# Folding the logits of a pair of tiles by two transposes and an add on VectorE

## What is computed

```python
x = x + 0.5 * ffn(layernorm(x));  x = x + attn(layernorm(x));  x = x + 0.5 * ffn(layernorm(x))

def ffn(input, weight, bias, centroids, assignments):      # 64 clusters
    dots = softmax(x @ centroids.T / 0.1, axis=-1)
    hits = dots > 0.01
    query_sel = any(hits, axis=1);  cluster_sel = any(hits, axis=0)
    row_sel = cluster_sel[assignments]
    out = where(query_sel[:, None] & row_sel[None, :], x @ weight.T + bias, 0)

def attn(x, Wq, bq, Wk, bk, Wv, bv):                       # 32 heads of 32, 8 of them for k and v
    scores = einsum('bsdh,bseh->bsde', q, k) / sqrt(32)    # per token, over the heads
    out = einsum('bsde,bseh->bsdh', softmax(scores, axis=-1), v)
```

## Time and profile before

| | us |
|---|---|
| median of 3 runs | 1257.59 |
| lowest and highest run | 1253.8, 1264.04 |
| span of the profiled execution | 1253.4 |
| TensorE busy | 1224.9 |
| TensorE weight loads busy | 1052.8 |
| VectorE busy | 841.3 |
| ScalarE busy, GpSimd busy | 411.3, 419.6 |

### The profile page before, as it was taken

One profiled execution on the slowest core, in us unless ns is written; L12 is line 12 of the kernel. 1 busy time (PEld: TensorE's weight loads), 2 busy tenths in 40 slices (PEclk: granted clock), 3 DMA queues, 4 the chain that ended last, 5 costly groups with the idle time before them and its releaser, 6 DMA issues.

```text
span 1253.4 us, 21699 instructions
## 1 busy us (share of the span) xinstructions
PE 1224.9 (98%) x8552; PEld 1052.8 (84%) x8552; DVE 841.3 (67%) x1207; ACT 411.3 (33%) x590; POOL 419.6 (33%) x551
## 2 busy tenths in 40 slices
PE   6999999999998899999999999999999999999998
PEld 5778888888887788888888888888888888887886
DVE  5644355345452378878788787887878865279887
ACT  4313222322210134443444444444444443212120
POOL 1225544543423634323333333333332200040322
PEclk8999999999998999999999999999999999999999
DMA  7376776776663345555555555455555554116785
GB/s 260 101 210 184 231 199 201 198 223 176 168 179 117 110 124 155 156 135 163 156 139 157 141 158 162 133 160 139 152 160 133 148 142 162 67 51 236 275 302 193
DMA packets 318693, 208.53 MB, mean 166 GB/s; under 512 B 258304, under 2 KB 281344, under 8 KB 318592
## 3 DMA queue, kind: packets, MB, share of 16 engines
q1 hardware_dynamic: 303712, 187.74, 52.0%
q10 hardware_dynamic: 14880, 19.40, 4.5%
HBM read 118.49 MB, written 88.60 MB: 165 GB/s over the span
## 4 chain that ended last, share of the span: by engine, by line
PE 90%; DVE 3%; DMA 2%; ACT 1%; issue 1%; SPq 1%; POOL 1%; POOLq 0%; DVEq 0%; ACTq 0%
PE ps_b L269 13%; PE ps_b L271 13%; PE ps_b L270 13%; PE ps_a L269 11%; PE ps_a L271 10%; PE ps_a L270 10%; PE ps_t L276 6%; PE ps_s L1348 5%; PE ps_s L283 2%; PE ps_s L285 2%; PE ps_s L1398 2%; PE ps_s L290 1%; DMA y_scratch<-xa 1%; SPq L398 1%; DMA ya_tok<-y_scratch 1%
## 5 line engine op out<-in xcount | busy, mean ns | idle before, releaser
L269 PE MATMUL ps_a<-w_hi,odd_hi 128*128 128x512 f32 x464 | 186.4, 402 | 0.0
L271 PE MATMUL ps_a<-w_hi,odd_lo 128*128 128x512 f32 x464 | 182.1, 392 | 0.0
L270 PE MATMUL ps_a<-w_lo,odd_hi 128*128 128x512 f32 x464 | 181.6, 391 | 0.0
L269 PE MATMUL ps_b<-proj_hi,y_hi 128*128 128x256 f32 (+1 forms) x512 | 177.7, 347 | 0.0
L271 PE MATMUL ps_b<-proj_hi,y_lo 128*128 128x256 f32 (+1 forms) x512 | 172.7, 337 | 0.0
L270 PE MATMUL ps_b<-proj_lo,y_hi 128*128 128x256 f32 (+1 forms) x512 | 172.0, 336 | 0.0
L303 POOL TENSOR_TENSOR var_eps<-moments,eps 128x1 f32<-128x1 f32 x96 | 18.4, 191 | 406.2 <-DVE moments L299 406.2
L661 POOL TENSOR_TENSOR x_ring<-x_ring,f_tmp 128x1024 f32<-128x1024 f32 x32 | 77.0, 2405 | 163.6 <-DVE probs L1112 135.4
L962 DVE TENSOR_TENSOR f_out<-ps_b,bias_a 128x512 f32<-128x512 f32 x30 | 20.7, 689 | 147.9 <-PE ps_b L271 147.9
L607 POOL TENSOR_SCALAR f_out<-f_out,token_on 128x1024 f32<-128x1024 f32 x30 | 85.6, 2854 | 88.3 <-DVE f_out L962 88.0
L271 PEld LDWEIGHTS ps_b<-proj_hi,y_lo 128*128 128x128 f32 x512 | 97.1, 190 | 10.8
(11 more groups left out here) (188 smaller groups left out, 2731.5 us busy)
## 6 DMA issues: line engine op xcount, KB each, us to landing
xa<-in_L_attn_x SPq DMA_DIRECT2D x32, 512.0 KB, 5.2
f_tmp<-f_scratch SPq DMA_DIRECT2D x32, 512.0 KB, 4.4
x_ring<-in_L_attn_x SPq DMA_DIRECT2D x32, 512.0 KB, 3.3
f_scratch<-f_out SPq DMA_DIRECT2D x30, 512.0 KB, 4.0
x_scratch<-x_ring SPq DMA_DIRECT2D x30, 512.0 KB, 3.3
y_scratch<-xa SPq DMA_DIRECT2D x28, 512.0 KB, 3.7
ya_tok<-y_scratch SPq DMA_DIRECT2D x112, 128.0 KB, 3.2
late<-x_scratch SPq DMA_DIRECT2D x22, 512.0 KB, 6.9
```

The source lines that it names most:

```text
L269: pe.matmul(acc, hi[:, k, :], w_h[:, k, cols], start=(k == 0), stop=False)
L270: pe.matmul(acc, hi[:, k, :], w_l[:, k, cols], start=False, stop=False)
L271: last = pe.matmul(acc, lo[:, k, :], w_h[:, k, cols], start=False, stop=(k == KB - 1))
```

## The change

The two matmuls of the fold become two transposes of 128x128 blocks. They turn the sums and leave the two halves beside each other, so `logit_ps` has 256 columns instead of 128. VectorE copies the first halves of both tiles from PSUM to `pair_exp_in`, adds the second halves from PSUM, and takes maximum and difference there, in SBUF. A pair's softmax has seven steps on `soft_step` instead of five, and `pair_soft_in` waits for the previous exponential before it writes `pair_exp_in`. The constant `fold` and the reduction that made it fall away.

```diff
-        fold = sb("fold", [P, NCL])
...
-        logit_ps = ps_s[:, HALF + 2 * P:HALF + 2 * P + 2 * NCL]
+        logit_ps = ps_s[:, HALF + 2 * P:EMB]
...
         def fold_logits(pe):
             for n in range(2):
-                last = pe.matmul(logit_ps[:, n * NCL:(n + 1) * NCL], pair_sums[:, n * P:(n + 1) * P], fold[:, :],
-                                 start=True, stop=True)
+                last = pe.transpose(logit_ps[:, n * P:(n + 1) * P], pair_sums[:, n * P:(n + 1) * P], ident[:, :])
             return last
...
-            logits = logit_ps.rearrange(BY_TILE, c=NCL)
+            parts = logit_ps.rearrange("p (t s c) -> p s t c", s=2, c=NCL)
+            logits = pair_exp_in[:, :].rearrange(BY_TILE, c=NCL)
             dve.wait_ge(folded, u + 1)
+            wait(dve, soft_exp, u)
+            dve.tensor_copy(logits, parts[:, 0]).then_inc(soft_step, 1)
+            dve.wait_ge(soft_step, 7 * u + 1)
+            dve.tensor_tensor(logits, logits, parts[:, 1], ALU.add).then_inc(soft_step, 1)
+            dve.wait_ge(soft_step, 7 * u + 2)
             dve.tensor_reduce(pair_max[:, :], logits, axis=AX.X, op=ALU.max).then_inc(soft_step, 1)
-            dve.wait_ge(soft_step, 5 * u + 1)
-            dve.tensor_tensor(pair_exp_in[:, :].rearrange(BY_TILE, c=NCL), logits,
-                              pair_max[:, :].unsqueeze(2).to_broadcast(PAIR), ALU.subtract).then_inc(soft_in, 1)
+            dve.wait_ge(soft_step, 7 * u + 3)
+            dve.tensor_tensor(logits, logits, pair_max[:, :].unsqueeze(2).to_broadcast(PAIR),
+                              ALU.subtract).then_inc(soft_in, 1)
...
-                dve.reduce_sum(fold[:, :], ident[:, :].rearrange("p (s c) -> p c s", s=2), AX.X)
```

More of the change, by code:

```diff
@@ L335, in pair_soft_out @@
             dve.reduce_sum(pair_sum[:, :], exp, AX.X).then_inc(soft_step, 1)
-            dve.wait_ge(soft_step, 5 * u + 2)
+            dve.wait_ge(soft_step, 7 * u + 4)
             dve.reciprocal(pair_inv[:, :], pair_sum[:, :]).then_inc(soft_step, 1)
-            dve.wait_ge(soft_step, 5 * u + 3)
+            dve.wait_ge(soft_step, 7 * u + 5)
             dve.tensor_tensor(exp, exp, pair_inv[:, :].unsqueeze(2).to_broadcast(PAIR), ALU.mult).then_inc(soft_step, 1)
-            dve.wait_ge(soft_step, 5 * u + 4)
+            dve.wait_ge(soft_step, 7 * u + 6)
             dve.reduce_max(pair_top[:, :], exp, AX.X).then_inc(soft_step, 1)
@@ L343, in pair_soft_out @@
             dve.tensor_tensor(best[n][:, :], best[n][:, :], pair_exp[:, :], ALU.max).then_inc(soft_done, 1)
-            dve.wait_ge(soft_step, 5 * u + 5)
+            dve.wait_ge(soft_step, 7 * u + 7)
             dve.tensor_scalar(token_on[n][:, 2 * p:2 * p + 2], pair_top[:, :], THRESHOLD, None, ALU.is_gt).then_inc(on_set, 1)
```

## The result

| | before | after |
|---|---|---|
| median, us | 1257.59 (7 runs, 1253.57 to 1264.04) | 1249.09 (7 runs, 1246.05 to 1251.5) |
| span of the profiled execution, us | 1253.4 | 1245.3 |

The ratio is 0.9933, with a 95% interval of 0.9909 to 0.9957: 8.5 us less where 6.0 were forecast.

The account below looks back on a forecast made before the run. TensorE was taken as the bound from 100 to 350 and 430 to 1060 us. The terms, 0.63 - 2.42 - 0.22 - 3.75 - 0.22, gave -6.0 us, so a median of 1251.6 us, range 1246 to 1259.

Parts of the forecast that it names:

- In the attention: Folds of pairs 16 to 30, behind small matmuls: 0.25 us saved each, between 0.22 and 0.33, in all -3.75 us.
- VectorE's price: A copy, an add and two waits per pair on VectorE cost 0.63 us, with ends of 0.50 and 0.75.
- the hole: First stage, pairs 2 to 13: VectorE idles 0.62 us behind the subtraction until ScalarE's cast, so the added work fits there.
- Pairs 13 and 14: Beside the stretch from 350.85 to 382.07 us: their savings are swallowed, TensorE's wait grows from 3.2 to 3.6 us; zero.
- Pair 15's own 0.22 us: The fold of pair 15, in TensorE's run from 382 to 394.9 us, was to save 0.22 us.
- The signs of being wrong: L940 following VectorE's own work later than now, new TensorE waits for low halves or scores, clock under 1.00 in long stretches.
- the startup's 0.63 us: First pair, softmax on the startup's chain: VectorE's added work isn't hidden and comes out whole at 70.62 us, +0.63.
- The clock falls more often: Rival: longer waits draw more clock drops of 1.7 or 2.0 us; one gives 1253.3 us; one to three 0.08, more 0.04.
- The rival's stronger form: Transposes don't count as work for the clock, each of 28 folds draws a drop: +42 us, 1299 us; within 0.04.
- Half of it arrives: Rival: a loop through a normed tile's store and reload carries the first stage, its 2.6 us are lost: 1254.2 us; 0.12.
- VectorE sets the pace: Rival, first stage: copy and add over 1.18 us pass the rest on; at 1.26 us, 1252.6 us in all; 0.04.
- No saving: Rival: each transpose comes out as two instructions like the matmuls, +0.6 us, 1258.2 us; 0.04.

Follow-up runs that it names:

- vector_alone: Against the kernel before: the fold stays two matmuls, VectorE does two more steps of the same size per pair; 1258.37 us, ratio 1.0007.
- vector_plus_four: The changed kernel with four further 128x128 VectorE steps behind the add of each pair; 1262.71 us, ratio 1.0048 to the kernel before.

## Why the prediction was right, and where it was off

**What bounds the kernel: right.** TensorE was the bound in both long stretches, and 0.22 us off a fold came off the period to the hundredth.

**The price of a fold in a product: right.** 0.22 forecast, 24.15 - 23.93 = 0.22 measured, and four transposes cost what four matmul instructions do.

**In the attention: a bit small.** 0.25 forecast, 0.29 measured, inside the ends of 0.22 to 0.33; 15 x 0.04 = 0.6 us. I took the lower half because a first weight load stays exposed. It does: two transposes and the product step behind them take 0.51 us there and 0.45 in the first stage. But the place is only 0.05 us dearer for transposes, where it was 0.10 for the matmuls, and some hundredths more come off elsewhere in the period. Why isn't shown.

**VectorE's price: right.** 0.63 forecast. From the first instruction of `pair_soft_in` to its subtraction it was 0.28 us and is 109.73 - 108.80 = 0.93: 0.65 more. The Trainium skill, "VectorE: DVE Perf Modes", in its section on the TRN2 errata, has (N + 151) cycles at 0.96 GHz for an fp32 add. An estimate from this for N = 128 is 291 ns; the median of the 32 adds is 289 ns, and the trace agrees.

**Where it lies: right in the three places that count.** In the first stage the hole swallowed it to within 0.01 us. In the attention the idle time fell from 1.57 to 0.66; I had written "by 0.6", and it fell by 0.91, since TensorE's scores come 0.28 us sooner too. In the startup pair 1 came 0.63 us later in its distance from pair 0, in every kernel that has just the change's work on VectorE in its place. That was sooner than forecast: I had the 0.63 us come out only at the wait that ended at 70.62 us. It shows at pair 1's logits already, as a new wait of 0.8 us for a low half, while the wait for pair 1's sums stayed at 2.1 us. The forecast for pair 2, 0.6 us later, fits (34.62 for 33.96 from pair 0), but the last piece scatters by 1 us.

**Pairs 13 and 14: right in kind.** The stretch from pair 14 to pair 15 swallowed the savings: 20.06 us before and 20.55 after, that is 0.5 longer where 0.22 was the forecast. Across the profiles it goes from 19.7 to 22.1 us, with a store and reload in it, so 0.3 us can't be read from one pair of profiles. Pair 15's own 0.22 us didn't show: from its logits to pair 16's it was 0.03 us more, not 0.22 less. From 395 to 412 us the chain isn't TensorE's, and this distance goes from 115.5 to 120.2 us across the profiles, so the pair is undecided.

**The signs of being wrong.** One of them came, twice: new waits for low halves, of 0.8 us at pair 1 and of 0.3 us at 262 us. The first is the startup's 0.63 us of the sum. The second had no term in the sum. Both are small, and the periods are those of the sum's mechanism. Another came in part: one of a pair's two low halves in the first stage waits no longer for ScalarE but follows VectorE's own work. It starts no later than before, though (2.36 us behind the transposes' start, before 2.35).

**The rivals.** *The clock falls more often* didn't happen: it stayed at 1.00 through both long stretches, and the runs lost less to it. Only one of the 14 profiles has a drop in either stretch, that of vector_alone, at 489 us, where one of the waits of 2.6 us ends. The rival's stronger form gave 1299 us; two transposes a fold at a clock of 1.00 and 1249.1 us speak against it, and so do four at 1.00 and 1255.8 us. The Trainium skill has it as a rule ("TensorE: Matmul & The Clock Gate", Part 4): transpose mode doesn't count as a busy TensorE. For a few transposes between matmuls the trace doesn't agree. *Half of it arrives*: in part. The reload of a normed tile now stops VectorE once or twice in the first stage in each of the three changed profiles, for 0.8, 0.8 and 1.8 us in all, and TensorE for 0.3, 0.3 and 1.2. It never does in the three profiles of before, but does in vector_alone, which has the old pace; it doesn't in the two of four transposes, which have the old pace and VectorE's added work as well. So what brings it on isn't shown. It costs 0.6 to 1.5 us of the 2.6, which the sum put at nothing. *VectorE sets the pace*: no, but the reserve was 0.15 us smaller than I had worked out. Of this, 0.05 is a time that stays between the low half's end and the matmul even when TensorE waits for it (124.82 and 124.87 us in vector_plus_four). *No saving*: no.

**The size: 6.0 forecast, 8.5 measured.** By the means of all runs the difference is 7.5 us; the other 1.0 is the scatter of medians of seven runs. Of the 7.5, 1.4 are less time at the lower clock, which the sum has no term for: I took the clock of before's one profile as given for both kernels. That leaves 6.1 us. That this is so close to 6.0 is in part luck, for two terms were off in opposite ways: the attention gave 0.6 us more, and the reload of a normed tile took 0.6 to 1.5 us that the sum doesn't have. The prediction's "some 3 us either way" for a median of few runs covers what happened.

## What to carry to other kernels

Where TensorE has no gap, price a change on it by the starts of its instructions and by how many instructions an operation comes out as: the fold was worth 0.22 us because four became two, and it came off every period. Find the hole on the helping engine before you fill it, and measure what is left of it with dummy steps: the first that comes through whole shows the edge (here 1.03 us), and that edge was nearer than the idle times added up (1.18 us). For a gain of half a per cent, compare a distance in the trace that comes many times over, with no wait at its end and no clock drop in it, and take its commonest value; it agreed to 0.01 us, while the gain by the medians' ratios went from 6.5 to 8.4 us.

## What the hardware showed that I had not expected

- Profiles of kernels that don't differ up to 36 us differ there by up to 1.9 us (L0 from 34.84 to 36.75), and the difference goes with a clock drop that lasts 0, 3.4 or 6.8 us. All drops in these profiles last 3.4 or 6.8 us, but for the one at the very end.
- In a product, four fp32 transposes of 128x128 take what two fp32 matmuls of 128x64 take (four instructions), 0.67 and 0.68 us with one product step, though they move twice the columns; behind the attention's small matmuls the transposes are 0.05 us cheaper at the fold and 0.10 us a period.
- A dependent step of 128x128 on VectorE costs 0.32 to 0.33 us from start to start, of which 0.29 are its own.
- A reload that comes late holds TensorE for 2.6 us once in 4 of 14 profiles, in kernels with and without the change.
